# A vision tower layer on one core: the first and last passes get an order of their own, written out call by call

## What is computed

```python
h = tok_ref(log_dt, Lambda, x, 1024)        # S4 kernel: sum over states of W * exp(P), h is 64 x 128 x 1024
h = h + attn_ref(layernorm(h), Wq, Wk, Wv, Wo)   # 128 tokens, 32 heads of 32, 8 kv heads, RoPE, causal softmax
h = h + ffn_ref(layernorm(h), A, B, Wr, br)      # 8 low-rank experts of rank 16, softmax router, scaled by 2
```

## Time and profile before

| | |
|---|---|
| median of 3 runs | 2428.21 us (2427.47 to 2428.85) |
| profiled execution | 2433.67 us |
| its span, first to last instruction | 2431.9 us |
| TensorE (PE) busy | 2298.0 us, 94% |
| VectorE (DVE) busy | 1984.0 us, 82% |
| ScalarE (ACT) busy | 1828.7 us, 75% |
| GpSimd (POOL) busy | 1709.9 us, 70% |
| mean granted TensorE clock | 0.983 of 2.4 GHz |

### The profile page before, as it was taken

How to read it: one execution, slowest core, us unless ns; L and a number is a source line. 1 busy time by engine, 2 the same in 40 slices (tenths; PEclk the granted TensorE clock), 3 DMA queues, 4 the chain that set the end, 5 groups by cost and what they waited for, 6 DMA issues and landing times.

```text
span 2431.9 us, 58560 instructions
## 1 busy us (share of the span) xinstructions
PE 2298.0 (94%) x18704; PEld 1249.2 (51%) x18704; DVE 1984.0 (82%) x7796; ACT 1828.7 (75%) x6270; POOL 1709.9 (70%) x1529
## 2 busy tenths in 40 slices
PE   2998489999999999999999999999999999999986
PEld 2777244555555555555555555555555555555543
DVE  8999468888888888888888888888888888888864
ACT  5988277777777787777777777777777777777773
POOL 1444087777777777777777777787777777777771
PEclk9999799999999999999999999999999999999997
DMA  2887389999999999999999999999999999999984
GB/s 67 265 252 241 109 150 177 185 186 187 185 190 181 191 187 184 184 190 190 185 183 189 185 183 189 188 186 184 190 186 185 186 190 188 179 193 181 185 163 98
DMA packets 1199524, 443.63 MB, mean 182 GB/s; under 512 B 1149552, under 2 KB 1151856, under 8 KB 1199216
## 3 DMA queue, kind: packets, MB, share of 16 engines
q1 hardware_dynamic: 1199216, 439.89, 91.3%
HBM read 87.42 MB, written 67.11 MB: 64 GB/s over the span
## 4 chain that ended last, share of the span: by engine, by line
PE 71%; ACT 6%; DVE 5%; DMA 3%; issue 2%; POOL 1%; SPq 1%; POOLq 0%; ACTq 0%; DVEq 0%
PE pb L852 8%; PE pa L852 8%; PE pb L853 8%; PE pb L854 8%; PE pa L854 7%; PE pa L853 7%; PE s_ps L866 4%; PE pc L852 4%; PE pc L853 4%; PE pc L854 4%; ACT pr L1004 4%; PE pv_ps L881 3%; PE pd L852 1%; DMA pt<-p 1%; PE pd L854 1%
## 5 line engine op out<-in xcount | busy, mean ns | idle before, releaser
L1004 ACT ACTIVATE pr<-pr,smin 128x128 f32<-128x128 f32 x2048 | 792.6, 388 | 191.1 <-DVE smin L1145 191.1
L1350 POOL TENSOR_TENSOR pr<-pr,rinv 128x512 f32<-128x512 f32 x512 | 576.9, 1137 | 355.8 <-DVE rinv L1153 345.2
L1358 POOL TENSOR_TENSOR p<-pr,p 128x512 f16<-128x512 f32 x512 | 590.1, 1158 | 117.8 <-ACT p L1014 111.3
L1145 DVE CUSTOM_DVE_ANT_0 pr<-s_ps,cst 128x128 f32<-128x128 f32 x2048 | 471.5, 286 | 150.3 <-POOL p L1358 107.2
L1014 ACT ACTIVATE p<-pr 128x512 f16<-128x512 f32 x512 | 319.0, 623 | 170.7 <-POOL pr L1350 150.9
L1004 ACT ACTIVATION_READ_ACCUMULATOR pr<-pr,smin 128x1 f32 x2048 | 382.2, 187 | 0.0
L611 PE MATMUL hps<-z,xw 128*128 128x256 f32 x848 | 194.7, 390 | 62.9 <-POOL xw L321 42.0
L852 PE MATMUL pa<-wkv_hi,xt 128*128 128x512 f16 x512 | 194.9, 381 | 28.5 <-DMA xt<-xs 28.5
L611 PEld LDWEIGHTS hps<-z,xw 128*128 128x128 f32 x848 | 163.5, 195 | 93.7 <-POOL xw L321 50.1
L866 PE MATMUL s_ps<-kt,qt 128*128 128x128 f16 x2048 | 199.1, 220 | 8.9 <-DVE smin L1145 5.0
L866 PEld LDWEIGHTS s_ps<-kt,qt 128*128 128x128 f16 x2048 | 149.5, 98 | 106.8 <-DVE smin L1145 5.8
(11 more groups left out here) (192 smaller groups left out, 5561.1 us busy)
## 6 DMA issues: line engine op xcount, KB each, us to landing
h<-hout SPq DMA_DIRECT2D x128, 256.0 KB, 3.8
h_ln<-h SPq DMA_DIRECT2D x64, 512.0 KB, 4.2
h_res<-h SPq DMA_DIRECT2D x64, 512.0 KB, 4.5
out<-h SPq DMA_DIRECT2D x64, 512.0 KB, 3.2
pt<-p SPq DMA_TRANSPOSE x512, 3.9
xa<-x SPq DMA_DIRECT2D x16, 256.0 KB, 4.1
xb<-x SPq DMA_DIRECT2D x32, 128.0 KB, 3.8
wst<-wq SPq DMA_DIRECT2D x8, 512.0 KB, 6.0
```

The source lines that it names most:

```text
L1004: last = A.activation(p, p, ACT.Exp, bias=smin[g % 2][:, j:j + 1], scale=-1.0, accum_out=rsum[g % 2][:, j:j + 1])
L1145: V.tensor_tensor_reduce(pr[g % 2][:, cols], s_ps[g % 2][:, cols], mask, 1.0, 3e38, ALU.add, ALU.min, smin[g % 2][:, j:j + 1]).then_inc(ma ...
L1350: nc.gpsimd.tensor_tensor(p3, p3, rinv[g % 2][:, :].unsqueeze(2).broadcast_to([P, HG, P]), ALU.mult).then_inc(p_norm, 1)
L1358: nc.gpsimd.tensor_tensor(p[:, HG * P:], pr[g % 2][:, :], p[:, 0:HG * P], ALU.subtract).then_inc(pl_done, 1)
```

## The change

The function body of each engine is kept as it is, and runs in a loop over the middle passes only (i from 10 to 54 on SP, 9 to 55 on TensorE, 9 to 54 on ScalarE and VectorE, 7 to 56 on POOL). In front of the loop and behind it the calls of the other passes are written out one by one, in an order of their own for each engine. The calls are the same ones, except that kv, q_half and wo_half are cut into other runs of k-steps (2757 calls on TensorE where there were 2752). The helper reached becomes upto, which gives the number to wait for, and three waits are new: kv waits for kv_used of the image before, q_half of half 0 for q_used of the image before, and wo_half for h1_done of the image before. The first stage stays as it is, with wo's parts in it. The diff, cut (the indentation too), with the beginning and the end of each engine's list:

```diff
-        def reached(eng, s, per, b, k=0):
-
-            if isinstance(b, int):
-                if b < 0 or per * b + k == 0:
-                    return
-                if b >= NB:
-                    b, k = NB, 0
-            eng.wait_ge(s, per * b + k)
+        def upto(per, b, k=0):
+
+            return 0 if b < 0 else per * NB if b >= NB else per * b + k
...
-        def bodies(eng, body):
-            for i in range(-3, NB + 3):
-                body(i, i % 2)
...
@@ -886,8 +1226,12 @@
         if not has(b):
             return
         if k0 == 0:
-            reached(pe, h1_done, 2, b - 3, 1)
-            reached(pe, xt_in, 16, b, 16)
+            if n := upto(2, b - 3, 1):
+                pe.wait_ge(h1_done, n)
+            if n := upto(1, b):
+                pe.wait_ge(kv_used, n)
+            if n := upto(16, b, 16):
+                pe.wait_ge(xt_in, n)
         last = products(pa[:, :], xt[odd], "wkv", slice(0, 512), k0, k1)
...
@@ -896,11 +1240,16 @@
         if not has(b):
             return
         if k0 == 0 and half == 0:
-            reached(pe, h1_done, 2, b - 3, 2)
+            if n := upto(2, b - 3, 2):
+                pe.wait_ge(h1_done, n)
+            if n := upto(2, b - 1, 1):
+                pe.wait_ge(q_used, n)
         if k0 == 0 and half == 1:
-            reached(pe, q_used, 2, b - 1, 2)
...
@@ -909,12 +1258,18 @@
     def wo_half(b, odd, half, k0, k1):
         if not has(b):
             return
+        if k0 == 0:
+            if n := upto(2, b - 1, half + 1):
+                pe.wait_ge(h1_done, n)
...
-    bodies(sp, body)
+    load_ln(0)
+    x_transpose(0, 0)
+    load_ln(1)
+    load_ln(2)
+    x_transpose(1, 1)
+    q_transpose(0, 0)
+    k_transpose(0, 0)
+    q_transpose(0, 1)
+    k_transpose(0, 1)
+    p_transpose(0, 0)
+    p_transpose(0, 1)
+    load_ln(3)
+    x_transpose(2, 0)
+    p_transpose(0, 2)
...
+    for i in range(10, 55):
+        body(i, i % 2)
...
+    x2_transpose(62)
+    store(61)
+    x2_transpose(63)
+    store(62)
+    store(63)
...
-    bodies(pe, body)
+    kv(0, 0, 0, 1)
+    q_half(0, 0, 0, 0, 1)
+    kv(0, 0, 1, 3)
+    q_half(0, 0, 0, 1, 8)
+    q_half(0, 0, 1, 0, 1)
+    kv(0, 0, 3, 6)
+    q_half(0, 0, 1, 1, 2)
+    kv(0, 0, 6, 8)
+    q_half(0, 0, 1, 2, 8)
+    kv(1, 1, 0, 1)
+    q_half(1, 1, 0, 0, 1)
+    kv(1, 1, 1, 4)
+    scores(0, 0)
+    q_half(1, 1, 0, 1, 2)
+    scores(0, 1)
+    q_half(1, 1, 1, 0, 1)
+    kv(1, 1, 4, 5)
+    q_half(1, 1, 0, 2, 4)
+    scores(0, 2)
+    kv(1, 1, 5, 6)
+    q_half(1, 1, 0, 4, 5)
+    kv(1, 1, 6, 7)
+    q_half(1, 1, 0, 5, 6)
+    q_half(1, 1, 1, 1, 2)
+    q_half(1, 1, 0, 6, 8)
+    kv(1, 1, 7, 8)
+    scores(0, 3)
+    scores(0, 4)
+    scores(0, 5)
+    q_half(1, 1, 1, 2, 5)
+    kv(2, 0, 0, 1)
+    scores(0, 6)
...
+    for i in range(9, 56):
+        body(i, i % 2)
...
+    scores(62, 7)
+    wo_half(61, 1, 0, 5, 6)
+    wo_half(61, 1, 1, 4, 5)
+    wo_half(61, 1, 0, 6, 7)
+    wo_half(61, 1, 1, 5, 6)
+    wo_half(61, 1, 0, 7, 8)
+    wo_half(61, 1, 1, 6, 8)
+    ls_transpose(60)
+    scores(63, 0)
+    wo_half(62, 0, 1, 0, 1)
+    scores(63, 1)
+    wo_half(62, 0, 0, 0, 1)
+    wo_half(62, 0, 1, 1, 2)
+    scores(63, 2)
+    scores(63, 3)
+    wo_half(62, 0, 1, 2, 3)
+    values(62, 1, 0)
+    wo_half(62, 0, 0, 1, 2)
+    out_half(60, 0)
+    scores(63, 4)
+    wo_half(62, 0, 0, 2, 4)
+    wo_half(62, 0, 1, 3, 5)
+    scores(63, 5)
+    out_half(60, 1)
+    wo_half(62, 0, 0, 4, 5)
+    scores(63, 6)
+    wo_half(62, 0, 0, 5, 6)
+    low(61)
+    scores(63, 7)
+    wo_half(62, 0, 0, 6, 7)
+    values(63, 0, 1)
+    wo_half(62, 0, 0, 7, 8)
+    wo_half(62, 0, 1, 5, 8)
+    wo_half(63, 1, 0, 0, 3)
+    wo_half(63, 1, 1, 0, 1)
+    ls_transpose(61)
+    wo_half(63, 1, 1, 1, 4)
+    out_half(61, 0)
+    out_half(61, 1)
+    values(63, 1, 1)
+    wo_half(63, 1, 0, 3, 5)
+    wo_half(63, 1, 1, 4, 5)
+    wo_half(63, 1, 0, 5, 8)
+    wo_half(63, 1, 1, 5, 8)
+    low(62)
+    ls_transpose(62)
+    out_half(62, 0)
+    out_half(62, 1)
+    low(63)
+    ls_transpose(63)
+    out_half(63, 0)
+    out_half(63, 1)
...
-    bodies(act, body)
+    norm_root(0, 0)
+    norm_apply(0, 0, None)
+    x_high(0, 0)
+    norm_root(0, 1)
+    norm_apply(0, 1, None)
+    x_high(0, 1)
+    q_high_a(0)
+    norm_root(0, 2)
+    v_high(0, 0)
+    k_high(0)
+    norm_apply(0, 2, None)
+    q_high_b(0)
+    x_high(0, 2)
+    exps(0, 0)
...
+    for i in range(9, 55):
+        body(i, i % 2)
...
+    ctx_high(63, 0, 1)
+    exps(63, 6)
+    exps(63, 7)
+    router_exp(61)
+    p_high(63, 6)
+    p_high(63, 7)
+    norm_root(1, 62)
+    ls_high(61)
+    norm_apply(1, 62, 0)
+    x_high(1, 62)
+    ctx_high(63, 1, 1)
+    norm_root(1, 63)
+    router_exp(62)
+    norm_apply(1, 63, 1)
+    x_high(1, 63)
+    ls_high(62)
+    router_exp(63)
+    ls_high(63)
...
-    bodies(dve, body)
+    norm1_stats(0)
+    norm_refine(0, 0)
+    x_low(0, 0, 0)
+    x_low(0, 0, 1)
+    norm1_stats(1)
+    norm_refine(0, 1)
+    x_low(0, 1, 0)
+    x_low(0, 1, 1)
+    q_rotate(0, 0)
+    norm1_stats(2)
+    q_double(0, 0)
+    kv_rotate(0)
+    norm_refine(0, 2)
+    k_double(0)
+    q_rotate(0, 1)
+    mask_min(0, 0)
+    q_double(0, 1)
+    mask_min(0, 1)
+    reciprocals(0, 0)
+    reciprocals(0, 1)
+    mask_min(0, 2)
+    x_low(0, 2, 0)
+    x_low(0, 2, 1)
+    reciprocals(0, 2)
+    q_rotate(1, 0)
+    mask_min(0, 3)
...
+    for i in range(9, 55):
+        body(i, i % 2)
...
+    residual1(61, 0, 1)
+    reciprocals(62, 7)
+    residual1(61, 1, 1)
+    mask_min(63, 0)
+    norm_refine(1, 61)
+    mask_min(63, 1)
+    q_double(63, 1)
+    reciprocals(63, 0)
+    ls_low(60)
+    reciprocals(63, 1)
+    mask_min(63, 2)
+    x_low(1, 61, 0)
+    mask_min(63, 3)
+    reciprocals(63, 2)
+    x_low(1, 61, 1)
+    residual2(60, 0, 0)
+    reciprocals(63, 3)
+    ctx_low(62, 1, 0)
+    mask_min(63, 4)
+    mask_min(63, 5)
+    reciprocals(63, 4)
+    reciprocals(63, 5)
+    mask_min(63, 6)
+    ctx_low(63, 0, 1)
+    mask_min(63, 7)
+    reciprocals(63, 6)
+    residual2(60, 1, 0)
+    router_max(61)
+    reciprocals(63, 7)
+    residual1(62, 0, 0)
+    router_weights(61)
+    residual1(62, 1, 0)
+    norm_refine(1, 62)
+    ls_low(61)
+    x_low(1, 62, 0)
+    x_low(1, 62, 1)
+    ctx_low(63, 1, 1)
+    residual2(61, 0, 1)
+    residual2(61, 1, 1)
+    residual1(63, 0, 1)
+    residual1(63, 1, 1)
+    router_max(62)
+    norm_refine(1, 63)
+    x_low(1, 63, 0)
+    x_low(1, 63, 1)
+    router_weights(62)
+    ls_low(62)
+    residual2(62, 0, 0)
+    router_max(63)
+    residual2(62, 1, 0)
+    router_weights(63)
+    ls_low(63)
+    residual2(63, 0, 1)
+    residual2(63, 1, 1)
...
-    bodies(pool, body)
+    sum_q(0, 0)
+    q_low(0, 0)
+    sum_k(0)
+    k_low(0)
+    sum_q(0, 1)
+    v_low(0, 0)
+    q_low(0, 1)
+    normalise(0, 0)
...
+    for i in range(7, 57):
+        body(i, i % 2)
...
```

More of the change, by code:

```diff
@@ new lines, in _ @@
+                reciprocals(2, 1)
+                norm_refine(0, 4)
+                mask_min(2, 2)
+                x_low(0, 4, 0)
+                x_low(0, 4, 1)
+                kv_rotate(3)
+                reciprocals(2, 2)
+                mask_min(2, 3)
+                ctx_low(1, 1, 1)
+                reciprocals(2, 3)
+                norm1_stats(5)
+                mask_min(2, 4)
+                x_low(1, 0, 0)
+                q_rotate(3, 1)
+                k_double(3)
+                reciprocals(2, 4)
@@ new lines, in _ @@
+                x_low(0, 5, 1)
+                reciprocals(3, 4)
+                ls_low(0)
+                residual2(0, 0, 0)
+                mask_min(3, 5)
+                norm1_stats(6)
+                q_rotate(4, 1)
+                q_double(4, 0)
+                residual2(0, 1, 0)
+                reciprocals(3, 5)
+                residual1(2, 0, 0)
+                residual1(2, 1, 0)
+                k_double(4)
+                mask_min(3, 6)
+                reciprocals(3, 6)
+                router_max(1)
@@ new lines, in _ @@
+                mask_min(5, 1)
+                kv_rotate(6)
+                x_low(1, 3, 0)
+                reciprocals(5, 1)
+                q_rotate(6, 0)
+                ls_low(2)
+                x_low(0, 7, 0)
+                mask_min(5, 2)
+                x_low(1, 3, 1)
+                mask_min(5, 3)
+                x_low(0, 7, 1)
+                reciprocals(5, 2)
+                residual2(2, 0, 0)
+                reciprocals(5, 3)
+                ctx_low(4, 1, 0)
+                mask_min(5, 4)
@@ new lines, in _ @@
+                mask_min(5, 5)
+                reciprocals(5, 4)
+                norm1_stats(8)
+                residual2(2, 1, 0)
+                q_double(6, 0)
+                reciprocals(5, 5)
+                q_rotate(6, 1)
+                residual1(4, 0, 0)
+                residual1(4, 1, 0)
+                mask_min(5, 6)
+                k_double(6)
+                mask_min(5, 7)
+                reciprocals(5, 6)
```

(110 more changed lines are left out.)

2492 lines of the change are left out of this document (2399 added, 93 removed).

## The result

The changed kernel takes 2432.99 us (median of 20 runs, 2428.99 to 2436.19) beside 2428.22 us for the kernel before (20 runs): ratio 1.0017, 95% interval 1.0011 to 1.0024. That is 0.17% slower, inside the 0.2% that I had called no change; by the medians it is 4.8 us, and the interval leaves out 1.0, so a little time was lost. I had predicted 2412 us. The profiled execution took 2435.99 us, its span is 2434.2 us.

A forecast was written before the change was run, and what follows sets the result against it. The prediction took TensorE as the bound, 99.7% busy in the middle, with waits and slow clock at both ends. Front 7.9 plus back 9.0 less 1.0 gave 16 us, so 2412 us at the median, range 2402 to 2425.

The forecast's parts named there:

- the last term: Images 2 to 8 and 56 to 61, the other passes with their own order: 1.0 us subtracted, from 0 to 6.
- the ring: Softmax of eight groups through two buffers; rival (0.10): it bounds new-order passes, slack 1.2 us a turn, 6 us lost.
- (b): Front, image 1: x_low moves ahead of the rotates, so TensorE's 4.18 us wait goes and kv(1) starts near 299.
- (c): Front, image 0: first mask at about 303 where it was at 312.0, so the ring starts 9 us earlier.
- (d): Front, the ring's first turns: remaining waits of TensorE, 6.0 us against 10.5.
- (i): Back: nine k-steps behind values(63, 1) start slow after some 7 us idle: 3 us, from 0 to 5.4.
- (e): Back: kv(63) and q(63) come earlier; mask of (63, 0) at T + 3, T ending the same prior TensorE work.
- (f): Back, image 63: three turns of the ring take 20.8 us, as before; no order of TensorE shortens them.
- (g): Back: mask (63, 6) to the end of values(63, 1) takes 11.8 us instead of 13.4.
- (h): Back: nine k-steps left behind values(63, 1), 1.4 and 5.2 us; before, sixteen and out(61), 14.6 us.
- slower: Rival (0.08): TensorE held in its own queue over 1 us in each of some sixteen passes, ending at 2433 to 2440.
- full DMA engines: Rival (0.08): DMA share 0.98 in the middle, so saved waits come back for pt or xt; 2424 to 2430.

The follow-up runs named there:

- e4: New order only up to image 1's softmax and from image 62's last groups, otherwise the order of before: 2415.45 us, ratio 0.9945 to the kernel before.
- e9: New order only up to image 0's softmax and from group 0 of image 62, otherwise the order of before: 2407.34 us, ratio 0.9912 to the kernel before.
- e12: The changed kernel with POOL's normalise on one head of four, other heads' probabilities left unnormalised: 2398.97 us, ratio 0.9872.
- e5: The changed kernel with 28 waiting TensorE calls (images 2 to 8, 55 to 61) moved behind the next two to four ready k-steps: 2429.92 us, ratio 1.0000.

## Why the prediction was wrong

I forecast 16 us less and it took 4.8 us more. The sum of my terms was 7.9 + 9.0 - 1.0; the ledger has 8.0 + 14.1 - 26.4, of which 25.2 lie in the two stretches next to the ends, and 2.2 of an earlier start that the change has no part in. Without that start the ledger gives +4.3 us, near the 4.8 of the medians.

**The step that failed** is the last term: "For the other passes with an order of their own (images 2 to 8 and 56 to 61) the trace of before shows nothing of the new interleaving. Nearest are the small waits of both lists; I subtract 1.0 us, from 0 to 6." It measures 25 us (12.7 in front, 12.5 at the back), four times its upper bound; e4 and e9 show that it is the order of these passes and nothing else, since with the order of before there the loss is gone and the wins stay. I bounded it by small waits of the kernel before. But those are the waits of an order that keeps TensorE 99.7% busy, and say nothing of an order that may not. My own sign of being wrong came true: TensorE waits for minima (1.4 and 1.9 us) and for transposed probabilities (1.2 and 0.8 us) from 400 to 600 and from 2150 to 2350, where the kernel before has no row for either.

**The assumption under it** was slack. I gave the ring 8.1 - 6.9 = 1.2 us a turn, and wrote of the middle that "no order of calls can give anything there". e12 shows that TensorE isn't clear of the ring in the middle either: with the leg 0.64 us shorter an image takes 32.29 us and not 32.64, which is 15 us in the ledger's middle. The lists of waits show little of it. From 600 to 2000 the changed kernel has these three rows, and e12 has none:

```profile
PE pb L1187 <- issue: 2.6, 4, 0.8
PE pa L1187 <- DVE ctx_t L2833: 2.0, 8, 0.4
PE pv_ps L1221 <- DMA pt<-p: 0.5, 1, 0.5
```

The starts of the matmuls tell more. Of the 15 us, 13.0 lie at the k-steps of wo that follow a call of scores: over the stretch 500-1800 the changed kernel loses 13.3 us between the last product of scores and such a k-step (7.5 us where the step goes into pb, 5.8 into pa), the kernel before 12.1, e12 0.3. They wait for VectorE: those into pa for ctx_low, and those into pb, in the kernel before, for q_rotate to have read the bank. The windows 600 to 2150 before, and 600 to 2120 in e12:

```profile
600.00:2150.00 1550.00, 1546.14 (x13239) 800.76 (x13238) 1297.93 (x5556) 1204.27 (x4234) 1197.16 (x1093) 1.00 0.99 186
```

```profile
600.00:2120.00 1520.00, 1519.67 (x13123) 793.65 (x13122) 1265.42 (x5501) 1194.22 (x4187) 954.03 (x1082) 1.00 0.97 189
```

TensorE lacks 3.9 us in the one and 0.3 in the other. The busy rows alone show a quarter of the 15 us; the rest was between matmuls that count as busy, since each shows 0.38 us and the next can start 0.22 us after it, so that up to 0.16 us of waiting doesn't show. The Trainium skill (page "Perfetto Trace Analysis", section Identifying the Most-Contended Engine) says that matmul busy share is not a good measure of how close a kernel is to its limit, because pipelined instructions look smaller in the trace. These rows agree that it is no good measure, but here the pipelined instructions cover waits, and TensorE looks busier than it is.

**The front came out as forecast, in part by luck.** (b) The wait for the transposed input of image 1 is gone: kv(1) follows q(0) without a gap, at 294.30 where I had 299. (c) The first mask starts at 298.12, and I had 303:

```profile
298.12 0.29 DVE L2817 CUSTOM_DVE_ANT_0 pr<-s_ps,cst 128x128 f32<-128x128 f32 x1 [1.77 <-PE s_ps L1204]
```

Of the 4.7 us at kv(1), 2.2 are the earlier start and 0.7 come from the transposing DMA of image 0, which landed 4.5 us after its issue and not 5.2. The other 1.7 are luck: the 24 k-steps of image 0 took 16.9 us where they had taken 18.7, because 7 of their matmuls were slow (0.6 us each) where 14 had been, and with this same front they take 16.9 to 18.5 us from profile to profile. (d) The waits of TensorE from 300 to 400 sum to 8.9 us and not to 6.0:

```profile
PE s_ps L1204 <- DVE smin L2817: 4.0, 2, 2.0
PE pa L1187 <- DMA xt<-xs: 2.2, 1, 2.2
PE pa L1187 <- issue: 1.9, 1, 1.9
PE pc L1187 <- DMA xt<-xs: 0.4, 1, 0.4
PE pb L1187 <- DVE h L2948: 0.4, 1, 0.4
```

The two that I had worked out are there: 2.03 us before scores(0, 5), where I had 2.4, and 2.15 us before kv(2), where I had 1.4. Those that I had not are 1.93 us before scores(1, 6) at 344.56 and 1.92 us before a k-step of wo(1) at 372.18; the first is one that (d) missed, the second belongs to the failed term. The clock in the windows from 300 to 360 lacks 3.6 us where it lacked 5.1: 1.5 given back and not 3.0. The 5.1 us that the rule of the Trainium skill (page "TensorE: Matmul & The Clock Gate", section Terms) prices in full came back only in part because both windows still show 0.94. In e9 both windows are at 1.00. Counted up to the work mark 60, the front's 8.0 us are 1.0 us until kv(0) begins (11.3 us after norm1_stats(0) and not 12.4), 4.5 of idle time (from 10.6 to 6.1) and 2.5 of faster matmuls, where I had 0.35, 4.5 and 3.0.

**The steps of the back held, and (i) was too careful.** The start T of what stands before scores(63, 0) is 2372.12 less its wait of 1.75, 2370.37. (e) The mask of (63, 0) is at T + 2.5, and I had T + 3. (f) The three turns take 19.8 us where I had 20.8:

```profile
2372.84 0.29 DVE L2817 CUSTOM_DVE_ANT_0 pr<-s_ps,cst 128x128 f32<-128x128 f32 x1
...
2392.61 0.29 DVE L2817 CUSTOM_DVE_ANT_0 pr<-s_ps,cst 128x128 f32<-128x128 f32 x1 [2.38 <-POOL p L3751]
...
2411.73 0.69 DVE L2948 SCALAR_TENSOR_TENSOR h<-pb,h_res 128x512 f32<-128x512 f32 x1 [0.52 <-PE pb L1189]
```

(g) From mask (63, 6) to the end of values(63, 1), at 2404.54, are 11.9 us (11.8 predicted). (h), (i) From there to the last residual1 are 7.2 us and not 9.6. The k-steps behind values(63, 1) start 0.65 us apart at full clock, where the earlier trace rows had 1.25: I expected TensorE to idle some 7 us ahead of them, but k-steps of wo(63) and out(61) fill that time, and it had last waited 2.32 us at 2397.38. The 3 us for a slow clock were 0. T to the last residual1 is 41.4 us, 45.2 predicted, 54.5 before; the chain behind it is 1.0 us shorter, and I had it 0.3 longer. So the back won 14.1 us, just over my upper bound of 14.

**The rivals.** The outcome is nearest to "slower", to which I had given 0.08: over 1 us in each of some sixteen passes, and 1.6 and 1.8 us an image is what was found. But its mechanism, TensorE held in its own queue, is not shown to be the cause: e5 moved 28 of those calls and got 4 us back. The ring, or POOL's queue that it shares, is a part of it (a quarter in front, half at the back, by e12). Nothing points to full DMA engines: their share falls from 0.99 to 0.93 where the time is lost (400 to 600), and TensorE's waits for a transfer there sum to 1.2 us. The Trainium skill's 261 GB/s for transposing DMAs (page "DMA: Bandwidth & Descriptors", section Latency and other measured facts), which the page gives for one kernel with a non-contiguous middle dimension, is untested here: on the profiles' pages no slice of the layer stage moves more than 197 GB/s.

**What stays open** is why the passes with their own order are 1.6 to 1.8 us longer. Three edits of one engine's order each, at places which the trace named, returned 4 us, 0 and less than 0. Giving one engine's whole order back alone was not tried; I expect that the engines would then wait for each other in a circle. What is shown is where it lies (images 2 to 9, 55 to 57, 60 and 61, by the pace), that no one wait in the lists accounts for it, and that the length of normalise is part of it.

## What to carry to other kernels

In this kernel the order that keeps the busiest engine at 99.7% in the steady state was worth keeping in every pass where the steady state's work is there. Write out by hand only the passes that lack a neighbour, and join the repeated order as early as it can be joined (here with images 1 to 61 in it: 21 us faster, where some nine passes of their own at each end gave nothing). A term for which the trace of before has no row should be bounded by what the critical engine would lose if the new order missed its rhythm (here 5% of those passes), and not by waits of the order that works. Before slack is claimed for a loop, shorten one leg of it and see whether the steady pace moves; here it did, by 0.35 us an image. And where matmuls overlap in the trace, look at their starts and not only at the busy share.

## What the runs showed of the hardware

The issue of the transposing DMA of image 0's input holds SP's queue for 1.44 us in all eleven profiles where it stands ahead of the next image's load, and for 3.43 to 3.57 us in the three where it stands behind it; the same transpose of image 1 holds it for 3.2 to 3.5 us in all of them, and those of all images for 1.3 to 4.9 us. I had carried 3.43 over as a fixed cost. In the changed kernel:

```profile
272.77 1.44 SPq L782 DMA_TRANSPOSE xt<-xs  x1
...
286.15 3.39 SPq L782 DMA_TRANSPOSE xt<-xs  x1
```

The first stage, the same in all of them, ends between 264.2 and 268.2 us (start of norm1_stats(0)), and the profile of before was the latest of all: part of its 5.5 us over the median is there. Of two profiled spans such a difference is to be taken off first.
